# A state-space scan kernel: dt's projections in pairs on two row tiles, B's transposes on a row tile, the mean square moved behind them

## The chip, the cores and the metric

The kernel runs on one core of a Trainium2 chip. The metric is the device time of one execution in microseconds (us); lower is better. The engines are named as in the profile: PE is TensorE (PEld its weight loads), DVE is VectorE, ACT is ScalarE, POOL is GpSimd, SP is SyncE.

## The reference, cut to what matters

Four Mamba layers run over 64 context rows and 512 rows of x for each of 16 batches, then a cross attention with an MLP. What the change touches lies in each Mamba layer:

```python
xz = jnp.einsum('bsd,ed->bse', rmsnorm(x, norm_w), ip_w)
xi, z = jnp.split(xz, 2, axis=-1)
...
xi = jax.nn.silu(conv.transpose(0, 2, 1))
xdbl = jnp.einsum('bse,fe->bsf', xi, xp_w)
dt, Bm, Cm = jnp.split(xdbl, [DR_, DR_ + DS_], axis=-1)
dt = jax.nn.softplus(jnp.einsum('bsr,er->bse', dt, dtp_w) + dtp_b)
dA = jnp.exp(dt[..., None] * A)
dBu = dt[..., None] * Bm[:, :, None, :] * xi[..., None]
# scan over time: h = dA*h + dBu, y = sum over the 16 states of h*C
```

The inner width is 512 (four chunks of 128 channels, c = 0 to 3), dt has rank 16, the state size is 16. All is float32.

## The kernel before, in words

**Order of the work.** A prefix of 8 steps (4 layers, two halves of the context) computes the states behind the context rows. Then come 4 blocks of 4 batches. A block has 16 main steps, n = 0 to 15 (4 layers times 4 batches), of 512 time rows each, and then attention and MLP of its 4 batches; the first projections of the next block (n = -2 and -1) are put between the MLP's jobs. The prefix's last step is interleaved with the first block's start in the same way.

**A main step** has 32 slots, v = 0 to 31. Each slot is a pair of states of one channel chunk. DVE runs two scans (`scan`, L1215). ACT makes their decays `exp(dt*A)` three slots ahead (`decay_of`, L889 and L892). PE makes the inputs dt*B*x of the next slot (`make_input`, L559: eight products on the two 64-row halves of the array, into four PSUM banks) and sums the products of the slot four behind (`sum_pair`, L578: sixteen 64-row transposes that accumulate; at the begin of a chunk also eight turns of the skip term, L572). POOL multiplies each pair of states with C (`product`, L1440).

**Jobs.** All other products of a step share two PSUM banks, the job banks 0 and 1. They are written into hand-made tables: MAIN_PE says in which slot PE does a job, MAIN_ACT, MAIN_DVE and MAIN_POOL say when the other engines take part, MAIN_BANK which bank a job uses (L46 and L71 to 88). A job waits until its bank's previous content has been read. In a slot, PE does the input of the next slot, then the sum, then the jobs (in slots 4, 12, 20 and 28 the jobs come ahead of the sum); ACT does y's eviction `yev` if there is one, then the decays, then its events. Every engine works through its queue in order, so a wait holds up all that stands behind it.

**The names that the change touches** (here `m` is the step whose work is done and n the running step, as `("dt2", 1)` means step n+1 and `("ms", 2)` step n+2):

- `xp` (slots 6 to 8) projects to `xdbl`: rows 0 to 15 hold dt, 16 to 31 C, row 32 is one (for the bias), rows 64 to 79 hold B. ACT evicts it (L1010).
- `bT` (slot 9, L632) transposes xdbl in four pieces to get B with time in the partitions; ACT copies the 16 columns of B out (L1017).
- `dt2`, `dt3`, `dt0`, `dt1` (slots 10, 11, 12, 13, L638) multiply rows 0 to 32 of xdbl with `dtw`; all four use bank 0, one after the other, and ACT copies each out in the same slot (L1025).
- `ms` (slot 11, L607) is the mean square of step n+2, in bank 1. ACT turns it into rstd in slot 13, behind dt1's copy: a table load (L949), Ln (L951), Exp (L953). DVE reads it in `norm0` and `norm1`, behind scan pairs 15 and 17.
- `soft` (slot 14) applies softplus with a table of its own; `carry` follows. `silu_z` (slot 2) ends with the load of the table LOG_EXP (L1001).
- `out0` (slots 15 to 17), `xi0` (slots 18 and 19) and `yt0` (slot 19, L648) come next on PE; DVE's `gate0` (L1250) waits for yt0.

Of the kernel before, what the change touches and what calls it, by code (L numbers as in the profile page):

```python
# [27 lines left out]
RING = 8  # L28
SLOTS_H = 12
ZS = 3  # L30
XP = 80
B_ROW = 64
HEADS, HD = 16, 16
HID = 4 * D
# [9 lines left out]
            "xi3": 1, "z0": 0, "z1": 0, "z2": 1, "z3": 1, "yt0": 0, "xp": 1, "yt1": 0, "bT": 1, "dt2": 0, "dt3": 0,  # L44
            "dt0": 0, "dt1": 1, "yt2": 1, "dxT0": 0}
MAIN_BANK = {"z0": 0, "z1": 0, "z2": 0, "z3": 1, "yt2": 0, "yt3": 1, "xp": 0, "dxT3": 1, "bT": 0, "ms": 1, "dt0": 0,  # L46
             "dt1": 0, "dt2": 0, "dt3": 0, "out0": 0, "xi0": 1, "yt0": 0, "dxT0": 0, "xi1": 1, "yt1": 0, "xi2": 1,
             "dxT1": 0, "out1": 0, "xi3": 1, "dxT2": 1}
PARTS = {"ms": KD, "xi": KD, "z": KD, "xp": KI, "out": KI}

# [19 lines left out]

MAIN_PE = {0: [("z1.1", 1)], 2: [("z2.0", 1), ("z2.1", 1)], 3: [("z3.0", 1)], 4: [("z3.1", 1)], 5: [("yt2", -1)],  # L71
# [130 lines left out]
def program(nc, xT, ctxT, w_early, ip_x, ip_z, xp_w, dt_w, op_w, a_log, d_par, pre_w1, pre_w2, cst,  # L202
            cst_attention, avec, wq, wk, wv, wp, w1, w2, b2, kept, c_rows, out):
    ctx = ExitStack()
    with ctx:
# [172 lines left out]
        def await_read_of(eng, ph, m, name):  # L378

            eng.wait_ge(job_read[ph.bank[name]], bank_free(ph, m, name) + 1)  # L380
# [166 lines left out]
        def _(pe):  # L547
# [36 lines left out]
            def job(ph, m, full):  # L584

                name, part = full.split(".")[0], full.split(".")[1:]
                parts = range(PARTS.get(name.rstrip("0123"), 1))
                if part:
                    parts = [parts[int(part[0])]]
                o, c, par = job_bank(ph, name), int(name[-1]) if name[-1].isdigit() else 0, m % 2  # L590
                if name[0] == "f":
                    pe.wait_ge(read_of(ph, name), bank_free(ph, m, name))
                    if name[1] == "m":
                        await_read_of(pe, ph, m, f"fq{c}")
                    else:
                        pe.wait_ge(fore.sem, fore.upto(ph.bk, f"sq{c}" if name[1] == "q" else f"sd{c}"))
                    for k in range(KD):
                        i = nc.tensor.matmul(o, ones_x, hT[:, c, k, :] if name[1] == "m" else fsq[k],  # L598
                                             start=k == 0, stop=k == KD - 1)
                    i.then_inc(job_done[ph.bank[name]], 1)  # L600
                    return
                if 0 in parts:
                    pe.wait_ge(read_of(ph, name), bank_free(ph, m, name))
                if name == "ms":
                    if ph.main():
                        pe.wait_ge(square_summed, ph.of(MAIN_STEPS, m + 1))
                        i = nc.tensor.matmul(o, ones_x, xn[:, 0, :], start=True, stop=True)  # L607
                    else:
                        pe.wait_ge(normed.sem, normed.at(ph, m, 1))
                        for k in parts:  # L610
                            i = nc.tensor.matmul(o, ones_x, xn[:, k, :], start=k == 0, stop=k == KD - 1)
                elif name[:2] == "xi":
                    if full in ("xi0", "xi0.0"):
                        pe.wait_ge(ipx_loaded, ph.layers(m) * 16)
                        await_read_of(pe, ph, m, "ms")
                    for k in parts:
                        i = nc.tensor.matmul(o, ipx[:, k, c * P:(c + 1) * P], xn[:, k, :], start=k == 0, stop=k == KD - 1)  # L617
                elif name[0] == "z":
                    if full in ("z0", "z0.0"):
                        pe.wait_ge(ipz_loaded, ph.layers(m) * 16)  # L620
                    for k in parts:
                        i = nc.tensor.matmul(o, ipz[:, k, c * P:(c + 1) * P], xn[:, k, :], start=k == 0, stop=k == KD - 1)  # L622
                elif name == "xp":
                    if 0 in parts:
                        pe.wait_ge(xpw_loaded, ph.layers(m) * 16)
                        pe.wait_ge(silu_x.sem, silu_x.at(ph, m, 1))
                    for k in parts:
                        i = nc.tensor.matmul(o[0:XP, :], xpw[:, k, :], xs[:, par, k, :], start=k == 0, stop=k == KI - 1)
                elif name == "bT":
                    await_read_of(pe, ph, m, "xp")  # L630
                    for b in range(NB):
                        i = nc.tensor.matmul(o[:, b * XP:(b + 1) * XP], xdbl[0:XP, b::NB], eye[0:XP, 0:XP],  # L632
                                             start=b == 0, stop=b == NB - 1, is_transpose=True)
                elif name[:2] == "dt":
                    if c == 2:
                        pe.wait_ge(dtw_loaded, ph.layers(m) * 16)
                        await_read_of(pe, ph, m, "xp")
                    i = nc.tensor.matmul(o, dtw[0:DR + DS + 1, c * P:(c + 1) * P], xdbl[0:DR + DS + 1, :],  # L638
                                         start=True, stop=True)
                elif name[:3] == "dxT":  # L640
                    pe.wait_ge(dtx_ready.sem, dtx_ready.at(ph, m, c + 1))
                    for b in range(NB):
                        i = nc.tensor.matmul(o[:, b * P:(b + 1) * P], dtx[:, b::NB], eye, start=b == 0, stop=b == NB - 1,
                                             is_transpose=True)
                elif name[:2] == "yt":
                    pe.wait_ge(y_out.sem, y_out.at(ph, m, c + 1))
                    for b in range(NB):
                        i = nc.tensor.matmul(o[:, b * P:(b + 1) * P], yT[:, c % 2, b * P:(b + 1) * P], eye,  # L648
                                             start=b == 0, stop=b == NB - 1, is_transpose=True)
                else:  # L650
                    if full in ("out0", "out0.0"):
                        pe.wait_ge(opw_loaded, ph.layers(m) * 16)
                        await_read_of(pe, ph, m, "yt2")
                    if c == 0 and KI - 1 in parts:
                        await_read_of(pe, ph, m, "yt3")
                    for k in parts:
                        i = nc.tensor.matmul(o, opw[:, k, c * P:(c + 1) * P], zs[:, m % ZS, k, :],  # L657
                                             start=k == 0, stop=k == KI - 1)
                if parts[-1] == PARTS.get(name.rstrip("0123"), 1) - 1:
                    i.then_inc(job_done[ph.bank[name]], 1)  # L660
# [211 lines left out]
        def _(act):  # L872
# [49 lines left out]
            def event(ph, m, name):  # L922
# [23 lines left out]
                    nc.scalar.activation(xn[:, :, :], hT[:, ph.slot(m), :, :], ACT.Square).then_inc(normed.sem, 1)  # L946
                elif name == "rstd":
                    o = job_bank(ph, "ms")
                    nc.scalar.preload_act_table_set(LOG_EXP)  # L949
                    await_done(act, ph, m, "ms")  # L950
                    nc.scalar.activation(o, o, ACT.Ln, bias=EPS).then_inc(normed.sem, 1)  # L951
                    act.wait_ge(normed.sem, normed.at(ph, m, 2))
# [59 lines left out]
                elif name == "bT":  # L1012

                    act.wait_ge(diag_ready.sem, diag_ready.at(ph, m - 1))
                    await_done(act, ph, m, name)
                    turned = job_bank(ph, name)[:, 0:NB * XP].rearrange("p (b s) -> p b s", b=NB)
                    nc.scalar.activation(xbc[:, par, :, :], turned[:, :, B_ROW:B_ROW + DS], ACT.Copy  # L1017
                                         ).then_inc(read_of(ph, name), 1)
                elif name[:2] == "dt":

# [485 lines left out]
        def _(sp):  # L1506
# [12 lines left out]
            def body(ph, n):  # L1519
# [14 lines left out]
                if 0 <= n < ph.steps - 1 and ph.slot(n) == last:  # L1534

                    await_done(sp, ph, n, "dt1")
                    sp.dma_start(dtw[0:DR + DS + 1, :], dt_w[ph.layer(m)]).then_inc(dtw_loaded, 16)
                if ph.main() and m < ph.steps:
                    sp.wait_ge(state.sem, state.at(ph, n))
                    sp.sem_inc(passed, 1)  # L1540
# [48 lines left out]
            def load_first_layer():  # L1589
                sp.dma_start(lv, w_early[0]).then_inc(lv_loaded, 16)  # L1590
                sp.dma_start(ipx, rows(ip_x[0])).then_inc(ipx_loaded, 16)
                sp.dma_start(ipz, rows(ip_z[0])).then_inc(ipz_loaded, 16)
                sp.dma_start(xpw, rows(xp_w[0])).then_inc(xpw_loaded, 16)
                sp.dma_start(dtw[0:DR + DS + 1, :], dt_w[0]).then_inc(dtw_loaded, 16)
                sp.dma_start(opw, rows(op_w[0])).then_inc(opw_loaded, 16)

            def load_rows(ph, b):
# [61 lines left out]
def _inputs(x, ctx_768, **w):  # L1659
# [18 lines left out]
    cst[:, 0:128] = p[:, None] == p[None, :]  # L1678
    cst[:, 128:256] = 1.0 / D
    cst[:, 256:320] = (p[:, None] % 64 == p[None, :64])  # L1680
    cst[DR + DS, 320] = 1.0
    cst[:, 321:353] = p[:32][None, :] // HD == p[:, None] // LC
    cst_attention = np.zeros((P, 392), np.float32)
    cst_attention[:, 0:128] = p[:, None] == p[None, :]
# [14 lines left out]
    xp_w[:, :, 0:DR] = xp[:, :, 0:DR]  # L1699
    xp_w[:, :, DR:DR + DS] = xp[:, :, DR + DS:]  # L1700
    xp_w[:, :, B_ROW:B_ROW + DS] = xp[:, :, DR:DR + DS]
    dt_w = np.zeros((L, DR + DS + 1, DI), np.float32)
    dt_w[:, 0:DR, :] = a(L0 + "dt_proj_w").transpose(0, 2, 1)
    dt_w[:, DR + DS, :] = a(L0 + "dt_proj_b")
    return {
        "xT": f(np.asarray(x).transpose(0, 2, 1)),
        "ctxT": f(np.asarray(ctx_768).transpose(2, 0, 1).reshape(DC, B * LC)),
# [28 lines left out]
```

## Time and profile before

| | |
|---|---|
| time, median of 3 runs | 8193.55 us (8185.39 to 8194.11) |
| time of the profiled execution | 8188.73 us |
| its span | 8186.7 us, mean granted clock 0.981 |
| PE busy | 7486.3 us (91%) |
| DVE busy | 6519.8 us (80%) |
| ACT busy | 5868.7 us (72%) |
| POOL busy | 6376.5 us (78%) |

How to read it: the shares are means over the prefix, the main steps and the attention. In the page's 40 slices PE, DVE and POOL all show 80 to 99% in the main steps, so no engine alone is the bound by its share, and the order of the waits in one step has to be read. A row of a timeline has the start, the time to the end of the last of its instructions, engine, line, operation, shapes and count, and in brackets the idle time ahead of it with what ended it.

### The profile page before, as it was taken

The numbers are of one execution on the slowest core, as the hardware profiler recorded it, in microseconds if no ns is written. First come the engines' busy times: TensorE is split into PE (matmuls) and PEld (weight loads), VectorE is DVE, ScalarE is ACT, GpSimd is POOL, SyncE is SP. The second block draws the span as 40 slices with busy tenths as digits, with TensorE's granted clock in tenths as the row PEclk, the third lists the DMA queues.
The fourth block names the chain that finished last, engine by engine and source line by source line (L and its number), as shares of the span: only waits on it lengthen the run. The fifth ranks groups of instructions, "written<-read, shape, count | busy, mean of one in ns | idle before, by whom it ended". The sixth has DMA issues, their size and how long they took to land. (4 is left out here: it accounts for less than half of the span.)

```text
span 8186.7 us, 204523 instructions
## 1 busy us (share of the span) xinstructions
PE 7486.3 (91%) x86656; PEld 5191.6 (63%) x86656; DVE 6519.8 (80%) x6490; ACT 5868.7 (72%) x10937; POOL 6376.5 (78%) x3556
## 2 busy tenths in 40 slices
PE   7888799999988899999988899999988899999989
PEld 4666466666664566666664666666664666666665
DVE  4888799999983499999983599999973699999972
ACT  5776677878774587887764678777864687778753
POOL 5986499999991499999980599999970699999960
PEclk8998899999999999999999999999999999999999
DMA  1111111111110111111110111111110111111110
GB/s 60 55 50 60 43 55 58 54 46 50 46 48 27 48 60 46 50 46 50 56 38 28 58 50 46 50 51 60 51 39 20 54 50 46 55 56 55 46 39 11
DMA packets 133326, 391.29 MB, mean 48 GB/s; under 512 B 49581, under 2 KB 78189, under 8 KB 95553
## 3 DMA queue, kind: packets, MB, share of 16 engines
q1 hardware_dynamic: 132416, 378.22, 12.9%
q8 instruction: 687, 11.26, 0.6%
q14 instruction: 223, 1.82, 0.1%
HBM read 364.93 MB, written 13.24 MB: 46 GB/s over the span
## 5 line engine op out<-in xcount | busy, mean ns | idle before, releaser
L1215 DVE TENSOR_TENSOR_SCAN arena<-arena,ps 128x512 f32<-128x512 f32 x4608 | 5340.8, 1205 | 597.7 <-issue 369.7
L1440 POOL TENSOR_TENSOR arena<-arena 128x1024 f32<-128x1024 f32 x2240 | 5259.1, 2375 | 419.6 <-DVE arena L1215 390.3
L559 PEld LDWEIGHTS ps<-arena 64*128 64x128 f32 x36864 | 2331.0, 190 | 1333.8 <-issue 765.5
L892 ACT ACTIVATE arena<-arena,rate 128x511 f32<-128x511 f32 (+1 forms) x4608 | 3036.3, 710 | 42.7 <-DVE arena L1215 42.0
L559 PE MATMUL ps<-arena 64*128 64x128 f32 x36864 | 2755.1, 286 | 267.0 <-DVE arena L1215 260.9
L578 PE MATMUL ps<-csts,arena 64*128 64x64 f32 x35840 | 1511.7, 223 | 28.0 <-POOL arena L1440 28.0
L578 PEld LDWEIGHTS ps<-csts,arena 64*128 64x128 f32 x35840 | 1426.9, 139 | 40.8 <-POOL arena L1440 33.9
L617 PE MATMUL ps<-arena 128*128 128x512 f32 x1152 | 629.8, 647 | 145.6 <-DVE arena L1245 138.6
L1449 POOL TENSOR_TENSOR arena<-csts,arena 128x512 f32<-128x512 f32 x576 | 609.5, 1060 | 81.1 <-ACT arena L1017 81.1
L889 ACT ACTIVATE arena<-arena 128x2 f32<-128x2 f32 x2048 | 405.2, 198 | 324.4 <-DVE arena L1215 317.3
L657 PE MATMUL ps<-arena 128*128 128x512 f32 x1120 | 602.2, 634 | 14.1 <-DVE arena L1250 6.2
L1245 DVE SCALAR_TENSOR_TENSOR ps<-arena,ps 128x512 f32<-128x512 f32 x576 | 425.9, 739 | 211.9 <-ACT ps L979 210.6
L622 PE MATMUL ps<-arena 128*128 128x512 f32 x1120 | 585.2, 628 | 9.6 <-DVE arena L1245 5.5
L969 ACT ACTIVATE arena<-arena 128x3 f32<-128x3 f32 x256 | 51.6, 202 | 686.0 <-PE ps L617 673.9
L1471 POOL TENSOR_TENSOR arena<-arena 128x512 f32<-128x512 f32 x288 | 372.1, 1292 | 170.9 <-ACT arena L1032 124.0
L686 PE MATMUL ps<-arena 128*128 128x512 f32 (+2 forms) x896 | 385.7, 573 | 2.5 <-ACT arena L1077 1.9
L1463 POOL TENSOR_TENSOR arena<-arena 128x512 f32<-128x512 f32 x64 | 82.4, 1287 | 385.2 <-ACT arena L946 385.2
L617 PEld LDWEIGHTS ps<-arena 128*128 128x128 f32 x1152 | 189.1, 193 | 286.9 <-DVE arena L1245 188.9
L1406 DVE TENSOR_TENSOR arena<-ps,arena 128x256 f32<-128x256 f32 x64 | 27.2, 424 | 396.4 <-PE ps L827 396.4
L638 PE MATMUL ps<-arena 33*128 33x512 f32 x576 | 314.3, 627 | 7.6 <-ACT arena L1025 7.6
L1025 ACT ACTIVATE arena<-ps 128x512 f32<-128x512 f32 x288 | 171.9, 597 | 173.4 <-PE ps L638 168.8
L686 PEld LDWEIGHTS ps<-arena 128*128 128x128 f32 (+1 forms) x896 | 164.8, 191 | 202.5 <-issue 200.5
(118 smaller groups left out, 6894.6 us busy)
## 6 DMA issues: line engine op xcount, KB each, us to landing
arena<-c_rows SPq DMA_DIRECT2D x288, 1024.0 KB, 4.8
arena<-ip_x SPq DMA_DIRECT2D x20, 512.0 KB, 4.3
arena<-ip_z SPq DMA_DIRECT2D x20, 512.0 KB, 4.2
arena<-op_w SPq DMA_DIRECT2D x20, 512.0 KB, 3.9
hT<-xT SPq DMA_DIRECT2D x16, 512.0 KB, 3.7
arena<-w SPq DMA_DIRECT2D x8, 1024.0 KB, 5.2
out<-arena SPq DMA_DIRECT2D x64, 128.0 KB, 1.7
arena<-xp_w SPq DMA_DIRECT2D x20, 160.0 KB, 2.5
```

What stands on the lines that cost most here:

```text
L559: i = nc.tensor.matmul(o, dtxT[half[h], c, b, :], diagB[half[h], pair, b, :].rearrange("p (i s) -> p i s", s=Q), start=True, stop=True)
L578: i = nc.tensor.matmul(acc[:, h, b * 64:(b + 1) * 64], hs[half[h], place(n, v) + s, b * P:(b + 1) * P], eye[half[h], half[h]], start=False ...
L617: i = nc.tensor.matmul(o, ipx[:, k, c * P:(c + 1) * P], xn[:, k, :], start=k == 0, stop=k == KD - 1)
L622: i = nc.tensor.matmul(o, ipz[:, k, c * P:(c + 1) * P], xn[:, k, :], start=k == 0, stop=k == KD - 1)
L657: i = nc.tensor.matmul(o, opw[:, k, c * P:(c + 1) * P], zs[:, m % ZS, k, :], start=k == 0, stop=k == KI - 1)
L686: last = nc.tensor.matmul(o, lhs, rhs, start=i == 0, stop=i == len(parts) - 1)
L889: nc.scalar.activation(dA[:, g % RING:g % RING + 2, 0:1], carried[:, n % 2, g:g + 2].unsqueeze(2), ACT.Copy)
L892: nc.scalar.activation(o, i, ACT.Exp, scale=rate[:, ph.layer(n), g:g + 1]).then_inc(decay.sem, 1)
L1215: nc.vector.tensor_tensor_scan(hs[:, place(n, v) + g % 2, :], dA[:, g % RING, :], pair[:, g % Q::Q], 1.0 if ph.main() else 0.0, ALU.mult, ...
L1245: i = nc.vector.scalar_tensor_tensor(o, w, taps[:, c, k:k + 1], acc_c, ALU.mult, ALU.add)
L1440: nc.gpsimd.tensor_tensor(hs[:, a:a + 2, :], hs[:, a:a + 2, :], Crep[:, 2 * pair:2 * pair + 2, :], ALU.mult).then_inc(prod.sem, 1)
L1449: nc.gpsimd.tensor_tensor(diagB[:, pair, :, :].rearrange("p b (i s) -> p b i s", s=Q), eye64.unsqueeze(1).unsqueeze(3).broadcast_to(shape) ...
```

## The change

The rows of dt and a second row of ones stand in xdbl twice, also in rows 80 to 96, behind B, and dt's weights stand in rows 80 to 96 too, with zeros ahead of them. So dt1 and dt3 can use rows 64 to 96. `dt2` and `dt3` are issued back to back in slot 10, `dt0` and `dt1` in slot 12, into banks 0 and 1; `ms` goes to slot 13, in bank 1. `bT` transposes rows 64 to 96 alone. The table load ahead of rstd is kept only in the prefix and for the first two steps of a block. The events of ACT keep their slots.

```diff
-XP = 80
+XP = 97
+DT_ROWS = DR + DS + 1
...
-             "dt1": 0, "dt2": 0, "dt3": 0, "out0": 0, "xi0": 1, "yt0": 0, "dxT0": 0, "xi1": 1, "yt1": 0, "xi2": 1,
+             "dt1": 1, "dt2": 0, "dt3": 1, "out0": 0, "xi0": 1, "yt0": 0, "dxT0": 0, "xi1": 1, "yt1": 0, "xi2": 1,
...
-           10: [("dt2", 1)], 11: [("dt3", 1), ("ms", 2)], 12: [("dt0", 1)], 13: [("dt1", 1)],
+           10: [("dt2", 1), ("dt3", 1)], 12: [("dt0", 1), ("dt1", 1)], 13: [("ms", 2)],
...
                 elif name == "bT":
                     await_read_of(pe, ph, m, "xp")
+                    rows = slice(B_ROW, XP)
                     for b in range(NB):
-                        i = nc.tensor.matmul(o[:, b * XP:(b + 1) * XP], xdbl[0:XP, b::NB], eye[0:XP, 0:XP],
+                        i = nc.tensor.matmul(o[:, b * DT_ROWS:(b + 1) * DT_ROWS], xdbl[rows, b::NB], eye[rows, rows],
                                              start=b == 0, stop=b == NB - 1, is_transpose=True)
                 elif name[:2] == "dt":
                     if c == 2:
                         pe.wait_ge(dtw_loaded, ph.layers(m) * 16)
                         await_read_of(pe, ph, m, "xp")
-                    i = nc.tensor.matmul(o, dtw[0:DR + DS + 1, c * P:(c + 1) * P], xdbl[0:DR + DS + 1, :],
-                                         start=True, stop=True)
+                    rows = slice(B_ROW, XP) if c % 2 else slice(0, DT_ROWS)
+                    i = nc.tensor.matmul(o, dtw[rows, c * P:(c + 1) * P], xdbl[rows, :], start=True, stop=True)
...
                     o = job_bank(ph, "ms")
-                    nc.scalar.preload_act_table_set(LOG_EXP)
+                    if not ph.main() or m < 2:
+                        nc.scalar.preload_act_table_set(LOG_EXP)
                     await_done(act, ph, m, "ms")
...
-                    turned = job_bank(ph, name)[:, 0:NB * XP].rearrange("p (b s) -> p b s", b=NB)
-                    nc.scalar.activation(xbc[:, par, :, :], turned[:, :, B_ROW:B_ROW + DS], ACT.Copy
+                    turned = job_bank(ph, name)[:, 0:NB * DT_ROWS].rearrange("p (b s) -> p b s", b=NB)
+                    nc.scalar.activation(xbc[:, par, :, :], turned[:, :, 0:DS], ACT.Copy
...
-                    sp.dma_start(dtw[0:DR + DS + 1, :], dt_w[ph.layer(m)]).then_inc(dtw_loaded, 16)
+                    sp.dma_start(dtw[0:XP, :], dt_w[ph.layer(m)]).then_inc(dtw_loaded, 16)
```

The loads of `xpw` (97 columns in place of 80) and `dtw` (97 rows in place of 33) grow with it; both come once a layer.

## Rows read from the trace of the kernel before

**Rows 1.** One steady step, from table load to table load: busy us of each engine.
```profile
3002.62:3097.01 94.39, 89.56 (x1164) 63.89 (x1161) 85.73 (x85) 75.26 (x147) 89.06 (x47) 1.00 0.13 48
```

**Rows 2.** Timeline of DVE, slots 10 to 20 of a steady step.
```profile
3084.43 6.86 DVE L1215 TENSOR_TENSOR_SCAN arena<-arena,ps 128x512 f32<-128x512 f32 x6 [0.74 <-issue]
...
3107.19 2.33 DVE L1215 TENSOR_TENSOR_SCAN arena<-arena,ps 128x512 f32<-128x512 f32 x2 [1.76 <-ACT arena L892]
...
3112.83 0.69 DVE L1250 TENSOR_TENSOR arena<-ps,arena 128x512 f32<-128x512 f32 x1 [0.49 <-PE ps L648]
```

**Rows 3.** Timeline of ACT, the same step: dt2's, dt3's, dt1's copies, table load, decays 18.
```profile
3087.99 0.60 ACT L1025 ACTIVATE arena<-ps 128x512 f32<-128x512 f32 x1 [0.90 <-PE ps L638]
...
3090.29 0.60 ACT L1025 ACTIVATE arena<-ps 128x512 f32<-128x512 f32 x1 [0.39 <-PE ps L638]
...
3096.39 0.60 ACT L1025 ACTIVATE arena<-ps 128x512 f32<-128x512 f32 x1 [0.50 <-PE ps L638]
3097.01 1.28 ACT L949 ACT_TABLE_LOAD   x1
...
3106.26 0.19 ACT L889 ACTIVATE arena<-arena 128x2 f32<-128x2 f32 x1
```

**Rows 4.** Timeline of PE, the same step, slots 9 to 19.
```profile
3084.16 0.66 PE L578 MATMUL ps<-csts,arena 64*128 64x64 f32 x16
...
3085.40 1.16 PE L559 MATMUL ps<-arena 64*128 64x128 f32 x16
3086.39 0.66 PE L578 MATMUL ps<-csts,arena 64*128 64x64 f32 x16
3086.88 0.65 PE L638 MATMUL ps<-arena 33*128 33x512 f32 x1
3086.89 0.48 PE L559 MATMUL ps<-arena 64*128 64x128 f32 x2
3087.37 0.59 PE L638 MATMUL ps<-arena 33*128 33x512 f32 x1
3087.80 0.94 PE L559 MATMUL ps<-arena 64*128 64x128 f32 x13
...
3090.18 1.12 PE L607 MATMUL ps<-arena,csts 128*128 128x512 f32 x2
3091.24 1.16 PE L559 MATMUL ps<-arena 64*128 64x128 f32 x16
...
3097.03 0.72 PE L578 MATMUL ps<-csts,arena 64*128 64x64 f32 x15
3097.54 1.16 PE L559 MATMUL ps<-arena 64*128 64x128 f32 x16
...
3109.58 1.16 PE L559 MATMUL ps<-arena 64*128 64x128 f32 x16 [0.56 <-DVE arena L1215]
```

**Rows 5.** Timeline of PE a step earlier: turns of the skip term, then the sum, in slot 28.
```profile
3048.22 0.46 PE L572 MATMUL ps<-csts,arena 64*128 64x64 f32 x8
3048.52 0.66 PE L578 MATMUL ps<-csts,arena 64*128 64x64 f32 x16
```

**Rows 6.** Timeline of PE: idle times and the work behind them.
```profile
3126.26 1.16 PE L559 MATMUL ps<-arena 64*128 64x128 f32 x16 [1.37 <-DVE arena L1215]
...
4220.68 1.98 PE L598 MATMUL ps<-arena,csts 128*128 128x512 f32 x4 [1.86 <-DVE arena L1287]
...
4646.16 1.16 PE L559 MATMUL ps<-arena 64*128 64x128 f32 x16 [2.03 <-DVE arena L1215]
...
6041.15 3.31 PE L598 MATMUL ps<-arena,csts 128*128 128x512 f32 x4 [1.86 <-DVE arena L1287]
```

**Rows 7.** Two stretches: busy us of each engine, granted clock (third number from the end).
```profile
6041.50:6044.90 3.40, 3.40 (x8) 1.17 (x8) 1.84 (x2) 1.39 (x3) 3.40 (x2) 0.52 0.02 5
4220.68:4224.08 3.40, 3.40 (x36) 2.16 (x36) 2.41 (x3) 2.68 (x7) 3.40 (x2) 1.00 0.00 0
```

**Rows 8.** Timeline of PE between the MLP's jobs, next block's dt0 (same at 4534.99, 4539.86, 4546.85).
```profile
4541.97 1.12 PE L638 MATMUL ps<-arena 33*128 33x512 f32 x2
```

More of the change, by code:

```diff
@@ L1593, in load_first_layer @@
                 sp.dma_start(xpw, rows(xp_w[0])).then_inc(xpw_loaded, 16)
-                sp.dma_start(dtw[0:DR + DS + 1, :], dt_w[0]).then_inc(dtw_loaded, 16)
+                sp.dma_start(dtw[0:XP, :], dt_w[0]).then_inc(dtw_loaded, 16)
                 sp.dma_start(opw, rows(op_w[0])).then_inc(opw_loaded, 16)
@@ L1680, in _inputs @@
     cst[:, 256:320] = (p[:, None] % 64 == p[None, :64])
-    cst[DR + DS, 320] = 1.0
+    cst[DR + DS, 320] = cst[XP - 1, 320] = 1.0
     cst[:, 321:353] = p[:32][None, :] // HD == p[:, None] // LC
@@ L1701, in _inputs @@
     xp_w[:, :, B_ROW:B_ROW + DS] = xp[:, :, DR:DR + DS]
-    dt_w = np.zeros((L, DR + DS + 1, DI), np.float32)
-    dt_w[:, 0:DR, :] = a(L0 + "dt_proj_w").transpose(0, 2, 1)
-    dt_w[:, DR + DS, :] = a(L0 + "dt_proj_b")
+    xp_w[:, :, B_ROW + DS:B_ROW + DS + DR] = xp[:, :, 0:DR]
+    dt_w = np.zeros((L, XP, DI), np.float32)
+    for r in (0, B_ROW + DS):
+        dt_w[:, r:r + DR, :] = a(L0 + "dt_proj_w").transpose(0, 2, 1)
+    for r in (DR + DS, XP - 1):
+        dt_w[:, r, :] = a(L0 + "dt_proj_b")
     return {
```

## The prediction

> **What bounds the kernel now.** I read first how regular the run is: ACT's table loads ahead of rstd follow each other at 94.39 us in the steady steps [rows 1]. I count n = 1 to 13 of each block as steady, 4 x 13 = 52 steps, some 60% of the span, so 0.01 us in one step is 0.5 us in the total. In such a step PE is busy 89.6, POOL 89.1, DVE 85.7 of 94.4 us [rows 1]: no engine has room, and none is the bound alone. So I followed who waits. From the middle of the step into slot 13 PE shows no idle time while DVE waits for inputs (0.74 us ahead of pair 10) [rows 2, 4]: PE sets the pace. ACT waits for each of dt's products (0.90, 0.39, 0.50 us) [rows 3]. Behind dt1's copy ACT runs without a gap through table load, rstd, softplus and carry to the decays of slot 18 at 3106.26 [rows 3], and DVE waits 1.76 us for these [rows 2]. Then PE waits 0.56 us for DVE's pair 18 [rows 4], and DVE 0.49 us for yt0 [rows 2]. So the end of a step hangs on PE up to dt1, on ACT up to the decays of 18, on DVE's pair 18, and on PE up to yt0.
>
> **The change, part by part.** The times of the steady step are kept as its clock.
>
> *B's transposes.* From the sum ahead of them to the next input it is 1.24 us [rows 4]; a sum leads to the next input in 0.51 (3097.03 to 3097.54) [rows 4], so bT costs 0.73. No row shows a transpose of 33 rows on the upper half alone. The nearest are the sums: sixteen 64-row transposes in that 0.51, eight on each half, 0.06 each, so four cost 0.25. The saving is 0 to 0.73; I take 0.48. dt2 then starts at 3086.88 - 0.48 = 3086.40.
>
> *The pairs.* dt2's two passes start at 3086.88 and 3087.37, and the lower half is free at 3087.80: 0.92 us [rows 4]. Two input products start at 3086.89, between the passes [rows 4]: these can only be on the other half, so the halves run side by side, and past instructions that stand ahead in the queue. A pair then costs 0.92; the other end is 2 x 0.92 = 1.84. I take 0.92, as the rows show the overlap. With dt3 and ms gone from slot 11, PE is early there, and DVE's pairs 13 and 14 no longer wait.
>
> *The mean square behind dt1.* This is the step that counts. Bank 1 now holds dt3, dt1 and ms in turn, so ms waits for ACT's copy of dt1. That copy keeps its place in ACT's queue, behind the copies of dt2, dt3 and dt0, two skip scalings, y's eviction and three slots of decays. From dt2's copy to dt1's it was 3096.39 - 3087.99 = 8.40 us, of which 0.39 + 0.50 were waits for PE [rows 3]: 7.5 us of work that nothing shortens. dt2's copy began 1.11 after dt2's start [rows 3, 4], now at 3087.5, so dt1's begins at 3095.0 and ends at 3095.6. ms takes 1.06 to the next input [rows 4], so input 15 starts at 3096.65, sum 10 0.99 later (as 3085.40 to 3086.39), and input 16, 0.51 behind it, at 3098.15; before it was 3097.54 [rows 4]. PE is 0.6 later, and its slack ahead of pair 18 was 0.56 [rows 4]: **the whole slack is used up, and the gain on PE is returned as a wait for ACT.** Behind ms on PE's queue stand the inputs of 15 and 16, for which DVE waits, and out0.
>
> *The table load.* It takes 1.28 [rows 3], is in 56 steps of the main blocks, and the table that it loads is already there since silu_z. ACT's chain gets shorter: rstd starts when ms ends, 3096.7, against 3098.3; decays 18 come 1.6 us earlier. DVE's pair 15 waits for input 15, about 0.5 later than before, but pair 18 no longer waits and starts near 3106.0, 1.2 earlier. That is worth nothing in a steady step, because yt0 now comes last: PE late by 0.6 less the lost 0.56. I set the steady step at 0.0, with bounds of 0.25 either way (the unknown bT and the 0.1 that neighbouring ACT operations overlap), 13 us in all.
>
> *Where PE has slack.* In the step n = 0 no out0 exists, and PE waits 2.03 us ahead of the same pair [rows 6]. There DVE's 1.2 us count: 4 x 1.2 = -5 us. Between the MLP's jobs, where PE is busy throughout, dt's products take 1.06 us each [rows 8]; two pairs in place of four products save 2.1, bT some 0.2, in 3 overlapped blocks: -7 us; the cover for the ms that now comes last is the MLP product between dt1 and ms. The prefix has no pairs in two banks, and there only bT counts: 0. The longer weight loads of SP, once a layer, wait for the same jobs (dt1 ends earlier) and land long ahead of use: 0.
>
> *The clock.* The wait ahead of ms has a second price. Pair 11 ends near 3089.0, so input 13 starts at 3089.1; 0.99 for it, 0.92 for dt0 and dt1, 0.30 for the turns [rows 5], 0.51 for sum 8, 0.99 and 0.51 for input 14 and sum 9: PE is done at 3093.4 and stands still until 3095.6, 2.0 us allowing for the modelled end of the last transpose. The trace has twelve idle times of 1.84 to 2.03 us behind inputs and sums or xi's products, three in each block (the first ends at 1003 us, the last at 7905; three of them stand in rows 6). Behind eight of them the granted clock falls to one half (1.2 of 2.4 GHz); 0.52 over 3.4 us in one stretch [rows 7]. The same work takes 3.31 us in place of 1.98 there [rows 6], and with the input behind it 1.65 more in all. After 1.37 us, which is in every steady step, it never falls: the step at clock 1.00 [rows 1, 6]. Of the four idle times behind xi's products two are followed by a fall, of the other eight six; the new one is in between, and I take 0.6. PE is the bound from ms to yt0, so the loss is in the step's time: 52 x 0.6 x 1.65 = +51 us. Bounds: none, and 0.9 of the steps, +77.
>
> **The sum** against the profiled execution: 8188.7 + 0 - 5 - 7 + 51 = 8228 us, slower by 0.5%. The profiled execution is 4.8 us below the median of the runs shown and inside their range, and I move nothing for that. A measurement of this kernel can tell about 0.2%, 16 us, from no change.
>
> **The rivals.**
>
> *The clock holds.* The idle time is somewhat shorter than I work out, or the streams of dt0 and dt1 shortly ahead of it keep the clock up. For it: four of twelve such waits had no fall, one of them the longest, 2.03 us [rows 6]. Against it: the same wait of 1.86 us, with the same work around it, once falls and once doesn't [rows 6]. Then the sum is 8188.7 - 12 = 8177 us, not slower. A fall in every seventh step (12 of 52 x 1.65 = 86 us) takes this gain away, and from a third of the steps on (28 of 86) the kernel is slower by what can be told.
>
> *The pair runs one after the other in part.* If dt3 has to start behind the second pass of dt2, a pair costs 0.49 + 0.92 = 1.41 us. dt1's copy does not move, ACT being late anyway, so only PE's idle time gets shorter, to 1.5 us, near the 1.37 that never let the clock fall. The time is again 8177. Against it: the order of starts in rows 4. The Trainium skill states this order as a rule (TensorE: Matmul & The Clock Gate, section Part 3, row and column tiling): matmuls start and end strictly in program order, only weight loads are pulled ahead. The trace of before disagrees, if the two products are those of the upper half, 0.48 us ahead of dt2's second pass.
>
> *ACT is faster than its rows.* If ACT's stretch is 0.5 us shorter, PE's lateness is 0.1 us, the 0.56 us of slack comes back, and the idle time falls to 1.5 us: 52 x 0.5 = 26 us more, 8151 us.
>
> *The load is put back.* Should the tool set a table load of its own ahead of Ln, ACT has 1.28 us more, and decays 18 come 0.3 us earlier than before in place of 1.6. DVE's pair 18 is then at 3106.9, still ahead of PE, and the time doesn't change; so this has no case of its own.
>
> **How the numbers follow.** The fall of the clock 0.50, the clock holds 0.28, the pair in part one after the other 0.14, ACT faster 0.08. The forecast's own range, with 0.25 to 0.9 of the steps, is 8198 to 8254. The range is 8166 to 8250: it takes in both cases at 8177 with most of their 13 us, and leaves out ACT faster, some of these low ends and the top. Slower: most of the first case, 0.45. 8177 is 0.15% below before, so of these 0.42 four tenths are faster, and with ACT's case faster is 0.25; the rest and the bottom of the first case are same, 0.30.
>
> **What would show it.** Right: in a steady step PE shows an idle time near 2 us ahead of L607, ended by ACT L1025; dt3's passes start with dt2's; DVE waits for yt0 some 1.7 us and no longer for decays 18; ACT waits about 1.1 us ahead of Ln; steps of 94.4 us stand beside steps of 96, with a granted clock near one half behind L607. Wrong: all steps alike at 94.4 and clock 1.00 (the clock holds); dt3's first pass at dt2's second (the pair); dt1's copy earlier than 7.5 us behind dt2's (ACT); or a first cause of waiting in another part of the step.

## The result, and the profile after

| | before | after |
|---|---|---|
| time, median of 5 runs each | 8188.57 us (8184.53 to 8194.11) | 8221.08 us (8216.76 to 8223.81) |
| profiled execution, span, mean granted clock | 8188.73, 8186.7 us, 0.981 | 8221.61, 8219.8 us, 0.970 |
| PE, ACT busy | 7486.3, 5868.7 us | 7447.5, 5786.3 us |
| ms waits for ACT's copy of dt1 | none | 109.8 us, 57 times |

After to before is 1.0037 [1.0026, 1.0048]: slower by 0.4%. PE and ACT have less to do, and the kernel takes longer. The line numbers of after are a little higher: L560 is the input, L579 the sum, L634 bT, L641 dt, L608 ms, L1028 dt's copies, L954 and L956 Ln and Exp, L1218 the scans, L1253 the gate.

Two successive steady steps of after, from softplus' table load to the next one (columns as in [rows 1]):

```profile
2911.33:3005.47 94.14, 87.88 (x1142) 63.52 (x1138) 84.43 (x84) 73.85 (x145) 89.47 (x47) 0.99 0.18 60
3005.47:3101.25 95.78, 89.53 (x1164) 65.09 (x1162) 85.47 (x85) 73.85 (x145) 89.11 (x47) 0.98 0.14 48
```

There are two sorts of step where before had one of 94.39. The shorter is 0.25 us better than before, the longer 1.39 worse. The longer sort pays for a fall: behind ms the granted clock goes from 1.00 to 0.50 for some 3 us. (The 0.99 of the first line is the beginning of such a fall, behind the ms at 3001.77; its cost lies in the second line.) A step that pays for none is called undisturbed here. The shorter sort first. PE in slots 9 to 15, and yt0 (L650), to be held against [rows 4]:

```profile
2896.39 0.66 PE L579 MATMUL ps<-csts,arena 64*128 64x64 f32 x16
2896.89 0.26 PE L634 MATMUL ps<-csts,arena 33*128 33x33 f32 x1
2896.89 0.37 PE L560 MATMUL ps<-arena 64*128 64x128 f32 x1
2896.98 0.41 PE L634 MATMUL ps<-csts,arena 33*128 33x33 f32 x2
...
2898.63 0.65 PE L641 MATMUL ps<-arena 33*128 33x512 f32 x1
2898.63 0.35 PE L579 MATMUL ps<-csts,arena 64*128 64x64 f32 x3
2898.82 1.07 PE L641 MATMUL ps<-arena 33*128 33x512 f32 x3
2899.54 1.13 PE L560 MATMUL ps<-arena 64*128 64x128 f32 x15
...
2907.63 1.12 PE L608 MATMUL ps<-arena,csts 128*128 128x512 f32 x2 [1.94 <-ACT arena L1028]
2908.68 1.16 PE L560 MATMUL ps<-arena 64*128 64x128 f32 x16
2909.68 0.66 PE L579 MATMUL ps<-csts,arena 64*128 64x64 f32 x16
2910.17 1.11 PE L560 MATMUL ps<-arena 64*128 64x128 f32 x16
...
2924.09 0.60 PE L650 MATMUL ps<-csts,arena 128*128 128x128 f32 x4
```

From the sum ahead of bT to dt2 it is 2.24 us (2896.39 to 2898.63), before 2.72 [rows 4]: bT costs 0.48 less, and its transposes lie beside the first products of the next input. The pair takes 0.91 to the next input, its four passes lie over one another. And then PE stands 1.94 us ahead of ms. ACT and DVE of the same step show who holds whom ([rows 2, 3] before):

```profile
2899.74 0.60 ACT L1028 ACTIVATE arena<-ps 128x512 f32<-128x512 f32 x1 [0.60 <-PE ps L641]
...
2907.00 0.58 ACT L1028 ACTIVATE arena<-ps 128x512 f32<-128x512 f32 x1
2908.79 0.58 ACT L954 ACTIVATE ps<-ps 128x512 f32<-128x512 f32 x1 [1.22 <-PE ps L608]
...
2916.75 0.19 ACT L891 ACTIVATE arena<-arena 128x2 f32<-128x2 f32 x1
```
```profile
2896.66 11.22 DVE L1218 TENSOR_TENSOR_SCAN arena<-arena,ps 128x512 f32<-128x512 f32 x10 [0.75 <-issue]
2909.95 2.33 DVE L1218 TENSOR_TENSOR_SCAN arena<-arena,ps 128x512 f32<-128x512 f32 x2 [2.07 <-issue]
...
2917.94 2.32 DVE L1218 TENSOR_TENSOR_SCAN arena<-arena,ps 128x512 f32<-128x512 f32 x2
...
2924.80 0.69 DVE L1253 TENSOR_TENSOR arena<-ps,arena 128x512 f32<-128x512 f32 x1 [1.72 <-PE ps L650]
```

ACT goes from dt2's copy to dt1's without a gap (7.26 us), ms waits for that copy, and ACT then waits 1.22 us for ms: the two engines take turns at standing still. DVE runs pairs 10 to 14 without a stop, as the earlier inputs promise, and waits 2.07 us for the input of slot 15, which stands behind ms on PE. Pair 18 waits for nothing now; yt0 comes last, and the gate waits 1.72 us for it.

Now the longer sort. The clock behind ms in the step at 3097.47 and, for comparison, in the step above (stretches of 1 us; granted clock third from the end):

```profile
3097.47:3098.47 1.00, 1.00 (x2) 0.30 (x2) 0.26 (x1) 0.00 (x0) 1.00 (x2) 0.96 0.00 0
3098.47:3099.47 1.00, 1.00 (x9) 0.87 (x10) 0.00 (x0) 0.73 (x2) 1.00 (x1) 0.50 0.00 0
3099.47:3100.47 1.00, 1.00 (x12) 1.00 (x12) 0.00 (x0) 1.00 (x3) 1.00 (x2) 0.50 0.00 0
3100.47:3101.47 1.00, 1.00 (x21) 1.00 (x20) 0.68 (x1) 0.98 (x3) 1.00 (x1) 0.50 0.00 0
3101.47:3102.47 1.00, 1.00 (x18) 1.00 (x18) 1.00 (x2) 1.00 (x1) 1.00 (x1) 0.83 0.00 0
```
```profile
2908.63:2909.63 1.00, 1.00 (x17) 0.95 (x18) 0.00 (x0) 0.81 (x2) 1.00 (x2) 1.00 0.00 0
2909.63:2910.63 1.00, 1.00 (x28) 1.00 (x28) 0.68 (x1) 1.00 (x4) 1.00 (x1) 1.00 0.06 16
```

Behind the same idle time 9 and 12 matmuls fall into two microseconds at half clock, where 17 and 28 did at full clock (an input's product counts as two). From ms to ms it is 94.14 us behind a step without a fall and 95.68 to 95.78 behind nearly all with one: a fall costs some 1.57 us. Of the 56 ms that follow an idle time of 1.94 or 1.95 us, 46 have the fall behind them and 10 don't.

### The profile page after: what moved, and what is told of

It is laid out like the page before. It is cut to its first block and busy times, and to the rows that moved or that the text cites. A ratio compares the mean times of both kernels' runs of the same rounds, so it can differ in the third digit from the quotient of the medians.

```text
span 8219.8 us, 204467 instructions
## 1 busy us (share of the span) xinstructions
PE 7447.5 (91%) x86656; PEld 5235.3 (64%) x86656; DVE 6502.6 (79%) x6490; ACT 5786.3 (70%) x10881; POOL 6373.2 (78%) x3556
## 5 line engine op out<-in xcount | busy, mean ns | idle before, releaser
L1218 DVE TENSOR_TENSOR_SCAN arena<-arena,ps 128x512 f32<-128x512 f32 x4608 | 5327.5, 1204 | 597.3 <-issue 474.9
L560 PEld LDWEIGHTS ps<-arena 64*128 64x128 f32 x36864 | 2389.4, 194 | 1276.9 <-issue 700.5
L560 PE MATMUL ps<-arena 64*128 64x128 f32 x36864 | 2788.5, 290 | 250.4 <-DVE arena L1218 244.3
L579 PE MATMUL ps<-csts,arena 64*128 64x64 f32 x35840 | 1539.9, 225 | 27.9 <-POOL arena L1443 27.9
L579 PEld LDWEIGHTS ps<-csts,arena 64*128 64x128 f32 x35840 | 1458.6, 141 | 40.4 <-POOL arena L1443 33.7
L1474 POOL TENSOR_TENSOR arena<-arena 128x512 f32<-128x512 f32 x288 | 372.4, 1293 | 126.9 <-ACT arena L1035 82.9
L1466 POOL TENSOR_TENSOR arena<-arena 128x512 f32<-128x512 f32 x64 | 82.8, 1294 | 385.7 <-ACT arena L948 385.7
L629 PE MATMUL ps<-arena 128*97 128x512 f32 x576 | 289.2, 611 | 1.8 <-ACT arena L989 1.7
L1498 POOL TENSOR_TENSOR arena<-arena 128x512 f32<-128x512 f32 x32 | 40.8, 1274 | 310.8 <-ACT arena L1170 310.8
```

What stands on the lines that cost most here:

```text
L560: i = nc.tensor.matmul(o, dtxT[half[h], c, b, :], diagB[half[h], pair, b, :].rearrange("p (i s) -> p i s", s=Q), start=True, stop=True)
L579: i = nc.tensor.matmul(acc[:, h, b * 64:(b + 1) * 64], hs[half[h], place(n, v) + s, b * P:(b + 1) * P], eye[half[h], half[h]], start=False ...
L1218: nc.vector.tensor_tensor_scan(hs[:, place(n, v) + g % 2, :], dA[:, g % RING, :], pair[:, g % Q::Q], 1.0 if ph.main() else 0.0, ALU.mult, ...
```

## The experiments

Eight kernels, in two groups. The kernel before ran beside each group, at 8189.69 us (8186.86 to 8193.06, seven runs) in the first and at 8190.19 us (8186.63 to 8194.85, nine runs) in the second; ratios are to it. Four questions: is it the clock, and the idle time ahead of ms? What are the parts worth alone? Why does the load bring nothing? What do the two halves bring?

### The idle time filled: one input made once more ahead of ms

```diff
                     for m, name in events("pe_at", ph, n, v):
+                        if ph.main() and name == "ms" and scans(ph, n):
+                            make_input(ph, n, v + 2, extra=True)
                         job(ph, m, name)
```

With `extra` the input announces nothing; it is made again at its place, so this kernel does 56 inputs more than after.

> The changed kernel with work added: ahead of the mean square PE makes input 15 once more, a result that is overwritten and waited for by nobody. The mean square still waits for dt1's copy. Clock theory: the idle time is cut into pieces of some 0.3 and 0.8 us, the clock stays at 1.00 behind it, all steady steps take the 94.14 us that the steps without a fall take now, and more work makes the kernel faster: 8221 less 43 falls times 1.57 us is 8150 to 8160 us. Rival (the wait itself or the work behind it costs the time): 8215 to 8235 us, no faster.

Measured: 8151.18 us (8150.75 to 8154.14), 0.9954 [0.9939, 0.9969]. The steady steps are 94.13 to 94.16 us, all but two of 94.5 us (a few steps of every trace, before too, are some 0.3 us longer and are left out of such ranges). ms, and the 5 us behind it (windows, as above):

```profile
2888.03 1.12 PE L609 MATMUL ps<-arena,csts 128*128 128x512 f32 x2 [0.75 <-ACT arena L1031]
```
```profile
2888.03:2893.03 5.00, 5.00 (x68) 3.74 (x69) 2.94 (x4) 3.77 (x7) 5.00 (x3) 1.00 0.02 5
```

PE has more work, ms starts no earlier behind dt1's copy, only the idle time is 0.75 in place of 1.94: no steady step has a fall, and the kernel is 70 us faster than after. This is the clock, shown by itself: 45 of the 52 steady steps at 1.57 us are 71 us.

### The pairs one after the other: all four products on rows 0 to 32

```diff
-                    rows = slice(B_ROW, XP) if c % 2 else slice(0, DT_ROWS)
+                    rows = slice(0, DT_ROWS)
```

> The changed kernel with all four projections of dt on rows 0 to 32: the pairs keep their slots and banks but both products of a pair are on the lower half of the array, one after the other. Clock theory: each pair takes 0.9 us more on PE, which only shortens the idle time ahead of the mean square to some 1.0 us; the clock stays up, steps of 94.14 us, 8150 to 8160 us: slower products, faster kernel. Rival (PE's work sets the end, the pairs' gain is real): two times 0.9 us in 52 steps come on top, 8260 to 8320 us.

Measured: 8154.21 us (8150.3 to 8160.13), 0.9957 [0.9943, 0.9972].

```profile
2885.92 1.12 PE L608 MATMUL ps<-arena,csts 128*128 128x512 f32 x2 [0.83 <-ACT arena L1028]
```
```profile
2885.92:2980.07 94.15, 89.01 (x1159) 63.88 (x1159) 85.57 (x86) 73.85 (x145) 89.45 (x47) 1.00 0.17 61
```

The slower products make the faster kernel: they fill 1.11 us of the same idle time (some 0.55 a pair, not the 0.9 that was expected), which was all that the two halves had bought there, and the clock holds: 1.00 over the step from ms to ms. Steps are 94.13 to 94.15 us here too, all but two.

### ms one slot later, behind the input of slot 15

```diff
-           10: [("dt2", 1), ("dt3", 1)], 12: [("dt0", 1), ("dt1", 1)], 13: [("ms", 2)],
+           10: [("dt2", 1), ("dt3", 1)], 12: [("dt0", 1), ("dt1", 1)], 14: [("ms", 2)],
```

> The changed kernel with the mean square one slot later (slot 14, behind input 15 and sum 10 on PE's queue), nothing else changed. Clock theory: input 15 (0.99 us) fills the wait for dt1's copy, PE's idle time falls from 1.94 us to some 0.5 in two pieces, the clock never falls behind it, and PE is 1.5 us ahead of the changed kernel's undisturbed step; decays 18 come last again, so a steady step is 92.5 to 93.5 us and the whole 8090 to 8130 us. Rival (the clock costs little; the time is in the wait for ACT): only the 1.5 us of PE that input 15 takes out of the wait are won, and the clock still falls: 8140 to 8170 us.

Measured: 8075.71 us (8074.04 to 8079.9), 0.9862 [0.9847, 0.9876]: 1.4% faster than before, the best kernel of this study. The undisturbed steady steps are 92.70 to 92.71 us. ms, pair 18 and the gate:

```profile
3054.72 1.12 PE L608 MATMUL ps<-arena,csts 128*128 128x512 f32 x2 [0.26 <-ACT arena L1028]
```
```profile
3064.77 2.33 DVE L1218 TENSOR_TENSOR_SCAN arena<-arena,ps 128x512 f32<-128x512 f32 x2 [1.27 <-ACT arena L894]
...
3070.45 0.69 DVE L1253 TENSOR_TENSOR arena<-ps,arena 128x512 f32<-128x512 f32 x1 [0.52 <-PE ps L650]
```
```profile
3054.72:3147.42 92.70, 88.14 (x1158) 63.59 (x1158) 85.47 (x85) 73.75 (x145) 88.97 (x47) 1.00 0.13 47
```

An input and a sum now stand where PE stood idle and fill 1.68 us of it, so only 0.26 us of the wait is left, the clock holds, and DVE gets the input of slot 15 without waiting. DVE waits for the decays of 18 again, as in [rows 2], but they alone do not set the end: PE shows no idle time from ms to yt0, and the gate waits 0.52 us for yt0. Against the undisturbed step of after this is 94.14 - 92.71 = 1.43 us, against the step with a fall 3.0. The step is as expected, the total below what was expected: 52 x 1.68 = 87 us (94.39 - 92.71 a step) account for 8102, and the rest is gained outside the steady steps, which the expectation left out: in the trace some 30 us, 13 of them in the three stretches between blocks and 11 up to the first n = 0 (after gains there as well, see the sum below).

### Of the change only the table load

The kernel before, with the load left out in the same 56 steps.

```diff
-                    nc.scalar.preload_act_table_set(LOG_EXP)
+                    if not ph.main() or m < 2:
+                        nc.scalar.preload_act_table_set(LOG_EXP)
```

> The kernel before with one part alone: the table load ahead of rstd left out in the same 56 steps. If ACT's chain from dt1's copy to decays 18 sets the end as predicted, decays 18 come 1.28 us earlier, of which PE's slack of 0.56 us lets 0.5 through in a steady step and all of it in the step n = 0: 26 to 31 us less, about 8158 us. Rival (ACT is hidden): 8188 us, no change.

Measured: 8147.44 us (8141.61 to 8149.27), 0.9947 [0.993, 0.9963]. A steady step, as in [rows 1]:

```profile
2906.93:3000.70 93.77, 89.45 (x1162) 63.89 (x1160) 85.72 (x85) 74.01 (x146) 89.42 (x47) 1.00 0.19 60
```

93.77 us in place of 94.39: the load alone is worth 0.62 us a step, half of its 1.28 and more than expected. In the kernel before it did stand on the chain. In the trace 31 us of the gain lie between n = 1 and n = 13, and 9 between n = 0 and n = 1.

### Of the change only B's transposes

dt's products, banks, the slot of ms and the load as before; bT on rows 64 to 96, with the wider xdbl and weights (the diff is cut to bT's own line).

```diff
-                        i = nc.tensor.matmul(o[:, b * XP:(b + 1) * XP], xdbl[0:XP, b::NB], eye[0:XP, 0:XP],
+                        i = nc.tensor.matmul(o[:, b * DT_ROWS:(b + 1) * DT_ROWS], xdbl[rows, b::NB], eye[rows, rows],
```

> Of the change only B's transposes on rows 64 to 96, with the wider xdbl and weights that they need; dt's products, the banks, the slot of ms and the table load as before. Theory (prediction): bT is 0.48 us shorter on PE at the place where PE sets the pace and ahead of ACT's chain that starts with dt2, so the step is 0.48 us shorter: 8190 - 52 x 0.48 = 8165 us. If bT runs wholly beside the next input, as the trace of the changed kernel has it, 0.73 us: 8152. Rival (covered elsewhere in the step): 8190 us.

Measured: 8164.62 us (8158.87 to 8170.99), 0.9968 [0.9956, 0.998]; undisturbed steady steps of 93.92 to 93.94 us. The sum ahead of bT and dt2:

```profile
3079.14 0.66 PE L579 MATMUL ps<-csts,arena 64*128 64x64 f32 x16
...
3081.38 0.65 PE L641 MATMUL ps<-arena 33*128 33x512 f32 x1
```

2.24 us as in after, and 0.46 of the 0.48 us comes through to the step, as forecast.

### The load put back, in after and with ms in slot 14

One edit on two kernels: the load ahead of rstd in every step again.

```diff
-                    if not ph.main() or m < 2:
-                        nc.scalar.preload_act_table_set(LOG_EXP)
+                    nc.scalar.preload_act_table_set(LOG_EXP)
```

> The changed kernel with the table load ahead of rstd in every step again (56 more loads of 1.28 us). Theory (the step as traced): ACT waits 1.29 us for ms between dt1's copy and Ln, so the load lies in that wait and costs nothing: 8221 us, 8205 to 8237, with the idle time of 1.9 us ahead of ms and the falls of the clock unchanged. Rival (the load is on ACT's chain to the decays of slot 18 here too, as it is in the kernel before, where leaving it out alone gave 0.62 us a step): 8221 + 56 x 0.62 = 8256 us.

> The version with ms in slot 14, in which the clock does not fall (8075.7 us), with the table load ahead of rstd in every step again. Theory: ACT waits 1.22 us for ms there as well, the load fills that wait, and the decays of slot 18 come 0.06 us later at most: 8076 us, 8070 to 8085, steps of 92.7 us. Rival: ACT's chain to the decays of slot 18, for which the scans wait 1.27 us, gets the load in part or whole: 56 x 0.62 to 56 x 1.28, 8110 to 8147 us.

Measured: 8222.63 us (8220.06 to 8227.31), 1.004 [1.0025, 1.0055], against 8221.08 without the load; and 8081.17 us (8077.34 to 8082.62), 0.9866 [0.9851, 0.988], with steps of 92.77, against 92.71. ACT behind dt1's copy in the first of the two:

```profile
2905.55 0.58 ACT L1027 ACTIVATE arena<-ps 128x512 f32<-128x512 f32 x1
2906.15 1.28 ACT L951 ACT_TABLE_LOAD   x1
2907.44 0.58 ACT L953 ACTIVATE ps<-ps 128x512 f32<-128x512 f32 x1
```

The load's 1.28 us lie in the time in which ACT waits for ms (1.22 in the rows above), and Ln starts 1.89 us behind the start of dt1's copy in place of 1.79, 0.10 later. So the loads cost next to nothing (1.5 and 5.5 us between runs of different groups; 0.06 us a step in the second, and nothing in the undisturbed step of the first), where they cost 42 us in the kernel before: moving ms behind dt1 put a wait in place of the load that the same change takes out.

### The two halves when the clock holds

ms in slot 14, all four products on rows 0 to 32.

> The version with ms in slot 14, but all four of dt's products on rows 0 to 32, one after the other in each pair. What are the two halves worth when the clock holds? Theory (PE is the bound from ms to yt0): the two pairs take 1.1 us more on PE (the idle time ahead of ms went from 1.94 to 0.83 us when this was done to the changed kernel), 0.26 us of it lies in the wait ahead of ms, the remaining 0.85 us is in the step: 8076 + 52 x 0.85 = 8120 us, 8105 to 8130, no wait ahead of ms. Rival (the decays of slot 18 set the end, and PE's lateness is covered by the 1.27 us that the scans wait for them): 8076 us, 8070 to 8085.

Measured: 8103.55 us (8096.03 to 8108.45), 0.9891 [0.9874, 0.9907]; steps of 93.24 us. ms and Ln:

```profile
2882.60 1.12 PE L608 MATMUL ps<-arena,csts 128*128 128x512 f32 x2
```
```profile
2883.76 0.58 ACT L954 ACTIVATE ps<-ps 128x512 f32<-128x512 f32 x1 [1.74 <-PE ps L608]
```

0.53 us a step, 28 us in all: between the two expectations. PE's lateness is felt, but the 1.1 us was too much: 0.26 + 0.53 = 0.79 us reach ms, and in the traces PE's stretch from dt2 to the last sum ahead of ms is 0.81 longer (8.89 in place of 8.08 us). My rival was wrong in its reason: the decays of 18 are no cover, since they hang on ms as well, by way of Ln, which now waits 1.74 in place of 1.22 us.

## Why the prediction was right, and where its terms were off

The forecast case came: slower, at 8221 where 8228 was given. Its steps, one by one.

**bT and the pairs** were right: 0.48 saved by the row, 0.46 a step in the run with bT alone. A sum, an input and a sum lead to dt2 in 1.99 us by [rows 4], so of the 2.24 bT costs the 0.25 that was worked out from the sums; that its transposes would lie beside the next input was not forecast. The first pair takes 0.91, the second 1.02 up to the turns behind it.

**ms behind dt1** was right in the mechanism and nearly in size: 1.94 us of idle time where about 2.0 was forecast, ended by ACT's copy; ACT's wait ahead of Ln 1.22 for 1.1; the gate's wait 1.72 for 1.7; none for the decays of 18. The term off is ACT's stretch from dt2's copy to dt1's, 7.26 us in place of 7.5: two neighbouring operations of ACT overlap by some 0.1 us (dt2's copy ends at 2900.34, the decays behind it start at 2900.23), but not where a wait stands between them, and I had taken off two waits without the overlap that returns. The second input behind ms comes 11.54 us after dt2's start (2898.63 to 2910.17), against 10.66 before [rows 4]: 0.88 later, where 1.09 was worked out. So the undisturbed steady step is 94.14, 0.25 below before, at the edge of the forecast 0.0 ± 0.25.

**The table load "worth nothing in a steady step"** holds, and the runs give a plainer reason than mine. I had it off the path because yt0 comes last. In truth it is off the path already at Ln, because ACT waits for ms nearly as long. Nor did I see that alone it was worth 0.62 us.

**The clock** decided, as forecast, and its share was the largest error: the fall follows 46 of 56 such idle times (45 of the 52 steady steps, 0.87), where I took 0.6 from twelve scattered cases [rows 6]. Its cost was 1.57 for 1.65.

**The sum.** Of the 33 us between the spans, the twelve intervals from n = 1 to n = 13 in each of the four blocks hold +53.9: 48 x -0.25 = -12, and so +66 of falls. From n = 0 to n = 1 it is -8.0 (forecast -5), in the three stretches between n = 14 and the next n = 0 -9.8 (forecast -7). That the latter two agree is luck: the three stretches hold -2.1, +0.2 and -7.8, where 2.3 was forecast for each, and with the pairs one after the other they still hold -6.9 in all, so it is not shown that the pairs gain there. Up to the first n = 0 it is -11.7, 6.3 of it beside the prefix's last step (from one table load ahead of rstd to the next 67.92 us, before 74.17): I had counted only three overlapped stretches and left out the first block's start. It is neither the load nor bT: in the runs of these alone this stretch is 1 to 2 us longer than before. All kernels with the new slots and banks of dt's products and of ms are 5 to 14 us shorter there; slots and banks were not tried alone. From n = 13 to n = 14, and at the end, it is +8.7, some 4 of it falls. The forecast of 51 for the falls was too small against +66, and so was -12 for all the rest against 33 - 66 = -33; the two errors have opposite signs, so that 8228 is nearer than its terms, by luck.

**The rivals.** "The clock holds" was 8177; with the clock held, by one input more, it is 8151, so this rival was right in its sign and 26 us high for the terms above. "One after the other in part" was wrong as a description of after, but its reasoning stands: the clock held behind a shorter idle time, 0.83 us (8154). The order of starts speaks against that description once more: bT's four transposes stand ahead of the next input in PE's queue, and yet the input's first product starts with the first of them and ahead of the other three (2896.89 against 2896.98). The Trainium skill (TensorE: Matmul & The Clock Gate, section Part 3, row and column tiling) has matmuls start and end strictly in program order; for the starts of products on two halves of the rows this trace disagrees. So what is said ahead of the prediction, that every engine works through its queue in order, does not hold for PE's starts between the two halves. "ACT is faster than its rows" came half true: the stretch is 0.25 us shorter and the step too, but the idle time is still 1.94 us and the clock falls. "The load is put back" was right that the time would not change, but not that the decays of 18 would come 1.3 us later: Ln comes 0.10 later.

**What the change would be worth** without its own side effect is now a sum of runs: bT 0.46 and the load 0.62 alone would bring about 93.3 us a step, if they add up, which was not run. The undisturbed step of after is 94.14; with ms one slot later it is 92.71, 1.68 below before, of which the two halves bring 0.53.

## What to carry to other kernels

A bank that is used in turn ties a product to whoever reads its last content: before moving a product, work out when that reader is done by its own engine's queue, not by when the product before it ends. Then look at what stands behind the moved product; where the bound engine would stand idle, put independent work there (here one input and one sum, 145 us between slots 13 and 14), for an idle time that recurs in every step can cost the clock too, and then work saved ahead of it makes the kernel slower. Price the parts of a change alone: the load and the transposes were worth 42 and 26 us by themselves, and together with the move the kernel lost 33.

## What the runs showed of the hardware that was not expected

The falls are not scattered but run in series. ms of after in four successive steps that end a series, each behind the same idle time (the second number is its duration):

```profile
3480.26 1.70 PE L608 MATMUL ps<-arena,csts 128*128 128x512 f32 x2 [1.95 <-ACT arena L1028]
3576.01 1.87 PE L608 MATMUL ps<-arena,csts 128*128 128x512 f32 x2 [1.94 <-ACT arena L1028]
3671.76 2.04 PE L608 MATMUL ps<-arena,csts 128*128 128x512 f32 x2 [1.94 <-ACT arena L1028]
3767.54 1.12 PE L608 MATMUL ps<-arena,csts 128*128 128x512 f32 x2 [1.94 <-ACT arena L1028]
```

From 1.12 at full clock ms grows step by step to 2.04, as the fall begins a little earlier in it each time; then comes a step without a fall (3767.54), and the next series begins. Three of the four blocks show this, with 2.08, 2.04 and 1.99 us at the end of the series; in the third block it ends at 1.66. The six other ms without a fall are those of n = 0 and 1 of the last three blocks. The trace with the load put back into after also has a fall behind 46 of 56, and in series too. So neighbouring steps are no independent draws, and a share read from scattered idle times was a poor guide. Why a series ends, and how short an idle time would still be followed by a fall, stays open: no run here lies between 0.83 and 1.94 us with the rest unchanged.
